# A two-layer LoRA kernel: V = A B by seven products of quadrants, and batch 0 like the others

## What is computed

```
x = x + (x W0^T + 0.5 (x A0[label]) B0^T)             W0 1024 x 1024, A0 5 x 1024 x 32, B0 1024 x 32
x = x + (x W1^T + bias + 2 (x A1[slot]) B1[slot])     W1 1024 x 1024, A1 24 x 1024 x 16, B1 24 x 16 x 1024
```

## Time and profile before

| | us |
|---|---|
| three runs | 327.05, 328.60, 329.57 (median 328.6) |
| profiled run, time | 328.35 |
| profiled run, span from first to last instruction | 326.5 |
| PE busy / DVE / ACT / POOL | 315.1 / 195.7 / 113.6 / 97.8 |
| mean granted clock of TensorE | 0.984 |

### The profile page before, as it was taken

The page is one execution under the profiler, slowest core; times in us unless marked ns, Lnnn a source line. Parts: engine busy times, 40 slices in busy tenths (PEclk is TensorE's granted clock), DMA queues, the critical chain, the costliest instruction groups (busy, mean ns, idle before and its releaser), DMA issues.

```text
span 326.5 us, 4679 instructions
## 1 busy us (share of the span) xinstructions
PE 315.1 (96%) x1593; PEld 277.2 (85%) x1593; DVE 195.7 (60%) x292; ACT 113.6 (35%) x188; POOL 97.8 (30%) x101
## 2 busy tenths in 40 slices
PE   5999999999999999959999999999999999999995
PEld 4999999999999998837878878878878878878874
DVE  1555461175163369979887578577577677666321
ACT  3344441131131103546724424424424425435110
POOL 2231120069352059317007016025024043052000
PEclk9799999999999999996999999999999999999999
...
GB/s 201 263 205 113 202 156 127 3 1 2 0 0 130 0 0 3 16 30 139 102 88 125 80 109 92 88 124 97 60 128 96 56 128 102 52 0 128 2 41 88
DMA packets 52596, 27.59 MB, mean 84 GB/s; under 512 B 31973, under 2 KB 48357, under 8 KB 52582
## 3 DMA queue, kind: packets, MB, share of 16 engines
...
## 4 chain that ended last, share of the span: by engine, by line
PE 87%; DVE 7%; DMA 2%; ACT 1%; issue 1%; SPq 1%; DVEq 0%; ACTq 0%
PE bank L859 85%; DVE t_sum L625 4%; PE bank L887 2%; DMA w_raw<-in_L_cond_W 2%; ACT p_hi L475 1%; DVE t_lo L625 1%; DVE xt L676 1%; DVE q L775 0%; SPq L264 0%; DVE p_lo L625 0%; DVE y L625 0%; DVE v_lo L625 0%; ACT v_hi L475 0%; SPq L258 0%; SPq L257 0%
## 5 line engine op out<-in xcount | busy, mean ns | idle before, releaser
L859 PE MATMUL bank<-r_hi,lhs_hi 128*128 128x384 f32 x192 | 65.2, 340 | 0.0
L859 PE MATMUL bank<-r_lo,lhs_hi 128*128 128x384 f32 x192 | 64.5, 336 | 0.0
L859 PE MATMUL bank<-r_hi,lhs_lo 128*128 128x384 f32 x192 | 54.1, 336 | 0.0
L625 DVE TENSOR_TENSOR v_lo<-bank,v_hi 128x384 fp32r<-128x384 f32 x24 | 12.4, 552 | 45.2 <-ACT v_hi L475 45.2
L859 PEld LDWEIGHTS bank<-r_hi,lhs_hi 128*128 128x128 f32 x192 | 36.4, 190 | 0.0
L859 PEld LDWEIGHTS bank<-r_lo,lhs_hi 128*128 128x128 f32 x192 | 36.3, 189 | 0.0
L859 PE MATMUL bank<-v_lo,lhs_hi 128*128 128x512 f32 x88 | 36.0, 409 | 0.0
L859 PEld LDWEIGHTS bank<-r_hi,lhs_lo 128*128 128x128 f32 x192 | 35.4, 189 | 0.0
L859 PE MATMUL bank<-v_hi,lhs_hi 128*128 128x512 f32 x88 | 35.4, 402 | 0.0
L859 PE MATMUL bank<-t_hi,s_hi 128*128 128x512 f32 x84 | 32.8, 390 | 0.0
L859 PE MATMUL bank<-t_lo,s_hi 128*128 128x512 f32 x84 | 32.8, 390 | 0.0
...
## 6 DMA issues: line engine op xcount, KB each, us to landing
...
```

The lines of the kernel that those rows point to most:

```text
L625: nc.vector.tensor_tensor(out_ap, one, other, op).then_inc(made, 1)
L859: return nc.tensor.matmul(ps, lhsT, rhs, start=start, stop=stop, skip_group_check=more)
```

## The change

All of stage V is new; the eight batches keep their scheme. V is made by the same seven products, on quadrants of 512 x 512 of A and B (P = 128, HK = 4 tiles each): M1 = A11 B11, M2 = A12 B21, M4 = A22 T4, M7 = S3 T3, M6 = S2 T2, M3 = S4 B22, M5 = S1 T1 in this order, where S1 = A21 + A22, S2 = S1 - A11, S3 = A21 - A11, S4 = S2 - A12, T1 = B12 - B11, T2 = B22 - T1, T3 = B12 - B22, T4 = B21 - T2. Each product has 4 row tiles x 4 steps x 3 = 48 matmuls of 512 columns. LOW are four banks, HIGH the other four; a row tile of a product takes one bank. M1 and M2 are summed in the banks, as V11. m1, m4 and w hold partial sums; v11, v21, v22 and vt1 to vt4 (sums of V's quadrants for the batches) are made from the banks.

a1's columns leave the product: c is made turned, as ct = a1^T A^T, in two halves (c_first and c_step, 24 matmuls of 512 columns each; the second with S1 and a1d, the difference of a1's halves), and turned by PE in 8 tiles. q is made in two halves of 16 matmuls of 512 columns, b0a1 in 16 of 128. b0_st has 12 tiles in place of 8 (the third four hold sums). w0 and w1 come by quadrants, in pieces of 256 KB (w1 in runs of 512 bytes, w0 of 2 KB), then the adapters' a1, then a22 and a21. Batch 0 is batch(0, True), with waits on V's parts. x is loaded by another view, in runs of 128 bytes where it had 1 KB, and turned by one DVE operation of 512 elements per quarter in place of two of 256; the rows within a batch are stored back to match. a0 comes by one DMA per batch in place of four.

ACT copies hi parts and raw banks. Its order after M2: v11_high, the raw b22 and v11, a1_hi, a1d_hi, q_part and p_hi, then t4_hi and a22_hi in turns, ct, t3_hi, s3_hi, m4, s1_hi, b22_hi, t2_hi, s2_hi, s4_hi, ct, c_hi, q, t1_hi; then x's quarters, vt3_hi and vt2_hi in turns, s_high, v21_hi and vt1_hi in turns, v22_hi, vt4_hi, and batch 0, which begins with a_high(0, 3).

The core of the diff. First SP and POOL, then DVE, then PE:

```diff
+                    src = x[bass.DynSlice(b, 1), :, :].rearrange("o (sl sb) (t i) -> sl (o sb t) i", sl=32, i=P)
+                    sp.dma_start(raw[32 * g:32 * g + 32, :].rearrange("p (st r) -> p st r", r=32),
+                                 src[:, :, 32 * g:32 * g + 32]).then_inc(x_in, 16)
...
+            pool.wait_ge(turned, 4)
+            for j in range(HK):
+                pool.wait_ge(w1_made, 2 * HK + j + 1)
+                pool.wait_ge(t1_made, j + 1)
+                tt(t2[:, j, :], b22[:, j, :], t1[:, j, :], ALU.subtract, t2_made)
+            for j in range(HK):
+                pool.wait_ge(a22_in[j // 2], 32)
+                add_eye_a(a22, j, w0_eyed)
+            pool.wait_ge(w0_eyed, 2 * HK)
+            for h in range(2):
+                pool.wait_ge(a21_in[h], 32)
+            pool.wait_ge(ct_done, 1)
+            tt(s1[:, PAIR[0], :], a21[:, PAIR[0], :], a22[:, PAIR[0], :], ALU.add, s1_made[0])
+            pool.wait_ge(w0_lo_made, HK)
+            for h in range(2):
+                pool.wait_ge(s1_made[h], 1)
+                tt(s3[:, PAIR[h], :], a21[:, PAIR[h], :], a11[:, PAIR[h], :], ALU.subtract, s3_made)
+            for h in range(2):
+                pool.wait_ge(s3_made, h + 1)
+                tt(s2[:, PAIR[h], :], s1[:, PAIR[h], :], a11[:, PAIR[h], :], ALU.subtract, s2_made)
+            pool.wait_ge(w0_lo_made, HK + HK)
+            for h in range(2):
+                pool.wait_ge(s2_made, h + 1)
+                tt(s4[:, PAIR[h], :], s2[:, PAIR[h], :], a12[:, PAIR[h], :], ALU.subtract, s4_made)
...
+            pool.wait_ge(v_done, M6 + HK)
+            sums(0)
+            for m in range(HK):
+                pool.wait_ge(vw_made, m + 1)
+                pool.wait_ge(vm4_made, m + 1)
+                tt(vt4[:, m, :], w[:, m, :], m4[:, m, :], ALU.add, vt4_made)
+                pool.wait_ge(vt4_made, m + 1)
+                tt(v21[:, m, :], m1[:, m, :], m4[:, m, :], ALU.add, v21_made)
...
+            def t1_t3(j):
+                dve.wait_ge(turned, 3 * HK + j + 1)
+                dve.wait_ge(w1_made, j + 1)
+                dve.wait_ge(w1_made, 2 * HK + j + 1)
+                tt(t1[:, j, :], TURN_BANK[j % 2][:, :], b11[:, j, :], ALU.subtract, t1_made)
+                tt(t3[:, j, :], TURN_BANK[j % 2][:, :], b22[:, j, :], ALU.subtract, t3_made)
...
+            v11_low(0)
+            v11_low(1)
+            t1_t3(0)
+            v11_low(2)
+            v11_low(3)
+            t1_t3(1)
+            t4_sum(0)
+            t1_t3(2)
+            t4_sum(1)
+            t1_t3(3)
+            dve.wait_ge(a1_in, 16 * B)
+            raw_a1 = a1_raw[:, :, :, :].rearrange("p t b r -> p t (b r)")
+            tt(a1d[:, :, :], raw_a1[:, HK:KT, :], raw_a1[:, 0:HK, :], ALU.subtract, a1d_made)
...
+            t4_sum(2)
+            q_half(0)
+            p_low(0)
+            t4_low(0)
+            a22_low(0)
+            t4_sum(3)
+            for j in range(1, HK):
+                t4_low(j)
+                a22_low(j)
+            dve.wait_ge(w0_eyed, 2 * HK)
+            dve.wait_ge(a21_in[1], 32)
+            dve.wait_ge(ct_done, 1)
+            tt(s1[:, PAIR[1], :], a21[:, PAIR[1], :], a22[:, PAIR[1], :], ALU.add, s1_made[1])
+            dve.wait_ge(b0a1_part_made, 1)
+            nc.vector.scalar_tensor_tensor(out=b0a1_all[:, :], in0=Q_BANK[0][0:R0, 0:G1], scalar=LORA0_SCALE,
+                                           in1=q_part[:, 0:G1], op0=ALU.mult, op1=ALU.add).then_inc(b0a1_all_made, 1)
+            for h in range(2):
+                dve.wait_ge(t_hi_made, T3_AT + h + 1)
+                low(t3_lo, t3, t3_hi, PAIR[h], t_lo_made)
+            for h in range(2):
+                dve.wait_ge(vs_hi_made, S3_AT + h + 1)
+                low(s3_lo, s3, s3_hi, PAIR[h], vs_lo_made)
...
+            for m in range(HK):
+                dve.wait_ge(vt3_hi_made, m + 1)
+                tt(vt3_lo[:, m, :], HIGH[m][:, :], vt3_hi[:, m, :].bitcast(F32), ALU.subtract, vt3_lo_made)
+                dve.wait_ge(v11_made, m + 1)
+                tt(vt2[:, m, :], HIGH[m][:, :], v11[:, m, :], ALU.add, vt2_made)
+                dve.wait_ge(vt2_made, m + 1)
+                dve.wait_ge(vy_made, m + 1)
+                tt(w[:, m, :], m1[:, m, :], vt2[:, m, :], ALU.subtract, vw_made)
+                dve.wait_ge(vt2_hi_made, m + 1)
+                dve.wait_ge(vw_made, m + 1)
+                low(vt2_lo, vt2, vt2_hi, m, vt2_lo_made)
             for j in (1, 0, 2, 3):
+                s_low(0, j)
+            for m in range(HK):
+                dve.wait_ge(v_done, M5 + m + 1)
+                dve.wait_ge(vt4_made, m + 1)
+                tt(vt1[:, m, :], LOW[m][:, :], w[:, m, :], ALU.add, vt1_made)
+                dve.wait_ge(v21_made, m + 1)
+                tt(v22[:, m, :], LOW[m][:, :], m1[:, m, :], ALU.add, v22_made)
+                dve.wait_ge(v21_hi_made, m + 1)
+                low(v21_lo, v21, v21_hi, m, v21_lo_made)
...
+            def step(ps, a, b, j, m, start, stop, more=False):
+                hi, lo = row_tile(a[0], j, m), row_tile(a[1], j, m)
+                mm(ps[:, :], hi, b[0][:, j, :], start, False, more)
+                mm(ps[:, :], hi, b[1][:, j, :], False, False, more)
+                return mm(ps[:, :], lo, b[0][:, j, :], False, stop, more)
...
+            def vm1(j):
+                pe.wait_ge(w1_lo_made, j + 1)
+                pe.wait_ge(w0_lo_made, j + 1)
+                for m in range(HK):
+                    last = step(LOW[m], A11, B11, j, m, j == 0, j == HK - 1)
+                    if j == HK - 1:
+                        last.then_inc(v_done, 1)
...
-            for pair in range(1, PAIRS):
-                pe.wait_ge(w0_lo_made, 4 * pair + 4)
-                for cs, e in (((0, 1), 0), ((0, 1), 1), ((2,), 0), ((2,), 1)):
-                    pe.wait_ge(v_lo_made, 6 * (pair - 1) + V_ORDER.index((e, cs[-1])) + 1)
-                    for k in range(KT):
-                        done = chunk_products([V_BANK[e, c][:, 0:BLK] for c in cs], pair % 2, pair_cols[e], k,
-                                              [blk[c] for c in cs])
-                    for d in done:
-                        d.then_inc(v_done, 1)
...
             warm_up(9)
+            turn_b11(0)
             warm_up(4)
+            turn_b11(1)
+            vm1(0)
+            turn_b11(2)
+            vm1(1)
+            turn_b11(3)
+            vm1(2)
+            turn_b21(0)
+            vm1(3)
+            turn_b21(1)
+            vm2(0)
+            turn_b21(2)
+            vm2(1)
+            turn_b21(3)
+            turn_b22(0)
+            vm2(2)
+            turn_b22(1)
+            turn_b22(2)
+            vm2(3)
+            turn_b22(3)
+            turn_b12(0)
+            pe.wait_ge(b0_lo_made, 1)
+            for j in range(HK):
+                q_step(Q_BANK[0], j, B11, j, j == 0, False)
+            turn_b12(1)
+            for j in range(HK):
+                last = q_step(Q_BANK[0], HK + j, B21, j, False, j == HK - 1)
+            last.then_inc(q_done, 1)
+            turn_b12(2)
+            turn_b12(3)
+            pe.wait_ge(a1_lo_made, 1)
+            c_first(0, A11)
+            c_first(1, A12).then_inc(ct_done, 1)
...
+            pe.wait_ge(q_made, 1)
             for k in range(KT):
+                mm(Q_BANK[0][:, 0:G1], b0_st[:, k, :], a1_hi[:, k, :], k == 0, False)
+                last = mm(Q_BANK[0][:, 0:G1], b0_st[:, k, :], a1_lo[:, k, :], False, k == KT - 1)
+            last.then_inc(b0a1_done, 1)
+            for j in range(HK):
+                pe.wait_ge(t_lo_made, T4_AT + j + 1)
+                pe.wait_ge(w0_lo_made, 2 * HK + j + 1)
+                for m in range(HK):
+                    if j == 0:
+                        pe.wait_ge(v11_made, m + 1)
+                    last = step(LOW[m], A22, T4, j, m, j == 0, j == HK - 1)
+                    if j == HK - 1:
+                        last.then_inc(v_done, 1)
+            pe.wait_ge(vs_lo_made, S3_AT + 2)
+            pe.wait_ge(t_lo_made, T3_AT + 2)
+            pe.wait_ge(t3_made, HK)
+            for m in range(HK):
+                if m == 2:
+                    pe.wait_ge(b0a1_all_made, 1)
+                if m == 3:
+                    pe.wait_ge(ct_made, 1)
+                row_product(HIGH[m], S3, T3, m, True, v_done)
+            pe.wait_ge(vs_lo_made, S1_AT + 2)
+            pe.wait_ge(a1_lo_made, 2)
+            pe.wait_ge(vm4_made, 1)
+            for j in range(HK):
+                c_step(C_BANK[1], (a1_hi[:, j, :], a1_lo[:, j, :]), S1, j, j == 0, False)
+            for j in range(HK):
+                last = c_step(C_BANK[1], (a1d_hi[:, j, :], a1d_lo[:, j, :]), A22, j, False, j == HK - 1)
+            last.then_inc(ct_done, 1)
+            pe.wait_ge(vm4_made, HK)
+            for j in range(HK):
+                q_step(Q_BANK[1], j, T3, j, j == 0, False)
+            pe.wait_ge(ct_made, 2)
+            for h in range(2):
+                for e in range(HK):
```

(83 more changed lines are left out.)

1132 lines of the change are left out of this document (554 added, 578 removed).

## The result

| | before | after |
|---|---|---|
| median of the runs | 327.8 us (327.0 to 329.6) | 340.2 us (339.7 to 340.8) |
| ratio to before | 1 | 1.037, 95% interval 1.032 to 1.042 |
| span of the profiled execution | 326.5 us | 339.0 us |
| matmuls, busy share of the matrix engine | 1593, 96% | 1397, 90% |

What follows compares the result with a forecast made beforehand. The matrix engine, 96% busy, bounds the kernel. The 22.3 us given back by matmuls, batch 0 and start are used up by three waits (22.1) and clock (9.0): span 335.5, +1.85 = 337.4 us; range 316 to 346.

Steps and rivals of the forecast that it cites:

- tail: Kernel's end, last add and store after the matmuls: 3.85 us, taken from the kernel before.
- clock behind the three waits: After the waits of c_first, M7 and M1: clock at 0.50, costing 3.0 us each, 9.0 in all.
- wait and start of c_first: Matrix engine waits 7.0 us for VectorE's a1_lo, made 12.8 us after the second product's end.
- wait and start of M7: After M4, matrix engine waits 4.8 us for s3_low's second, 38.6 us after the second product's end.
- wait and start of M1: Batch 0's first product waits 10.3 us for v22 of all four rows, behind VectorE's queue.
- The matrix engine's own sum: Matmuls removed 108.1 us, added 94.3 and 2.6 us: gain 11.2 us.
- One sign: Profile sign ahead of M7: VectorE's t3_lo and s3_lo at 3.3 us in place of 1.2.
- The five pairs: Ahead of M7: GpSimd's and VectorE's SBUF operations alternate, 5 pairs x 3.4 = 17.0 us.
- the walk: The prediction's step through both engines' queues, counting every collision; ahead of M7 it gave a 4.8 us wait.
- A faster c_first wouldn't help: Ahead of M7: VectorE's t4_low and a22_low would then fall into the same turns with GpSimd.
- No further wait: Batch 0's u_product: remaining lows and a_low(0, 3) end about 8.3 us after v22, so wait 0.
- Rival (b): Clock stays up after the waits for S3 and V: 6.0 us less, 331.4; chance 0.17 with a too-long walk.

Runs made afterwards that it cites:

- e11: A small kernel of its own, only adding tiles of zeros on VectorE and GpSimd, alone and together; back to back, a pair takes 2.8 us (512) or 3.3 (1024).
- e7: Against the kernel after: S's seven sums, x's first four and V's eight moved from GpSimd to VectorE; 331.3 us, ratio 1.012.
- e10: Against the kernel after: only the twelve sums behind M6 (x's first, V's vt4 and v21) moved from GpSimd to VectorE; 338.7 us, ratio 1.034.
- e2: Against the kernel after: batch 0's M1 waits for row 0 of vt1 and v22 only, M6's product for row 1, M5's for all; 342.0 us, ratio 1.041.
- e5: Against the kernel after: narrow waits of batch 0's first products, plus VectorE's order ahead of batch 0 changed; 341.0 us, ratio 1.041.
- e6: Against the kernel after: VectorE's half of s1 placed behind a22_low(1) instead of a22_low(3); 346.7 us, ratio 1.057.
- e3: Against the kernel after: a1d and a1_lo right behind t1_t3(1), a1d_lo behind t1_t3(2), instead of behind t1_t3(3); 337.4 us, ratio 1.028.
- e4: Against the kernel after: 60, 40 and 95 turns of eye on the matrix engine inside the three waits; 339.2 us, ratio 1.035.
- e1: Against the kernel after: each last-batch store split into four DMAs over sb, its outermost dimension of size 4; 334.8 us, ratio 1.020.

## Why the prediction was right

It was right in sign and size, and in the main by its own mechanism: three waits on VectorE, in these places, with a low clock behind each. That the sum comes so near is partly luck, since a tail 4.5 us too short stands against a clock 2.3 us too dear. Its terms, as forecast and as measured (E, the end of the second product, is 34.75 as measured; the tail counts from the end of the matmuls):

| step | forecast | measured |
|---|---|---|
| E, the second product's end | 34.8 | 34.75 |
| wait and start of c_first | 7.0, E+12.8 | 6.67, E+12.5 |
| wait and start of M7 | 4.8, E+38.6 | 4.54, E+37.1 |
| wait and start of M1 | 10.3, E+105.4 | 10.59, E+104.4 |
| wait of u_product | 0 | 1.00 |
| clock behind the three waits | 3.0 each | 1.7, 3.1, 1.9 |
| end of batch 0 | E+132.0 | E+131.1 |
| seven batches | 7 x 23.55 | 7 x 23.55 |
| tail | 3.85 | 8.3 |

- *The matrix engine's own sum.* Batches 23.55 us apart and batch 0 in 26.7 with 1.0 of wait and 1.9 of clock are as worked out. The start is right too: vm1(0) at 7.37 for 7.4, 1.2 us of half speed for 1.7, and E within 0.1.
- *The waits.* Prices from the earlier trace rows put all three within 0.4 us. e11 shows the price itself; e7 and e10 show that GpSimd's work on S, which holds VectorE and is held by it, makes M7's wait, and mostly VectorE's own queue M1's (e7: 8.99 us left with no GpSimd beside it). One sign failed in the kernel after: t3_lo and s3_lo take 1.2 us, only the last 2.27, not 3.3; held were the short operations ahead of them. The five pairs did not alternate one by one; what GpSimd lost in idle time it gained in not being held. In e2, e5 and e10 the sign is there, and M7 waits 2.9 to 3.9 us. So the walk's 4.8 is a little long and its nearness to 4.54 partly luck. e6 shows what the order can cost: 6.4 us by moving one operation.
- *Small slips.* By the prediction's own terms M7 starts at 21.3 + 17.0 = 38.3, not 38.6, and M1 at 73.3 + 31.8 = 105.1, not 105.4; 0.3 us each, which changes nothing.
- *"A faster c_first wouldn't help"* was wrong in the time: e3 gave 2.9 us, 3.8 up to M1. At M7 it is 1.0, and that is nearly as the prediction had it; the rest is that a wait of 1.25 us left the clock up where one of 4.54 didn't, which I had not weighed.
- *"No further wait" at u_product*: 1.0 us, and it stands by only because the clock was low (e4, where it is 2.8).
- *The clock.* 6.7 us lost, not 9.0. Rival (b), the clock holds, did not come about; e4 shows that it would have been worth about 1 us, not 6, as most is covered. The low stretch is not a fixed price: behind M7's wait it is 6.2 us in the execution shown and 3.0 in e1's, with the same code.
- *x.* Hidden, as forecast; the issue takes SP 5.44 us, not 9.76: the price by packets of 64 bytes was too high for 128. The stores, whose layout follows x's, cost 4.5 us at the end; the tail was taken over from before (3.85) without a look at them, and this is the term that was mis-sized most. Without these 4.5 the profiled execution would be at 336.3, 1.1 under the forecast; with them it is at 340.8.
